# Tokens' statistics in parts, the last attention steps in another order, and no fills behind GpSimd's gathers

## What is computed

```python
def ffn(x, Wr, br, W1, b1, W2, b2):            # xf: 4096 tokens x 128
    expert = argmax(xf @ Wr.T + br, -1)
    h = relu(einsum('td,efd->etf', xf, W1) + b1[:, None, :])    # 8 experts, 512 wide
    y = einsum('etf,edf->etd', h, W2) + b2[:, None, :]
    return y[expert, arange(4096)]
def attn(x, wq, wk, wv, wproj, g_rms):
    q, k, v = heads of x @ wq.T, x @ wk.T, x @ wv.T
    q, k = rope(g_rms * q / rms(q)), rope(g_rms * k / rms(k))
    return softmax(q @ k.T / sqrt(8) + 1) @ v @ wproj.T
x = x + 0.5 * ffn(layernorm(x)); x = x + attn(layernorm(x)); x = x + 0.5 * ffn(layernorm(x))
```

## Time and profile before

| | |
|---|---|
| median of 3 runs | 461.86 us (461.74 to 462.61) |
| the profiled execution | 463.23 us, its span 461.4 us |
| PE busy | 419.0 us, 91% of the span |
| DVE busy | 374.3 us, 81% |
| ACT busy | 350.3 us, 76% |
| POOL busy | 327.3 us, 71% |
| stages by the timeline | routing to 33; pass 1 to about 140; steps 0 to 64 to about 378; pass 2 to 457; last scatter lands at the end |

### The profile page before, as it was taken

The page is one execution under the profiler, slowest core; times in us unless marked ns, Lnnn a source line. Parts: engine busy times, 40 slices in busy tenths (PEclk is TensorE's granted clock), DMA queues, the critical chain, the costliest instruction groups (busy, mean ns, idle before and its releaser), DMA issues.

```text
span 461.4 us, 13980 instructions
## 1 busy us (share of the span) xinstructions
PE 419.0 (91%) x4123; PEld 313.4 (68%) x4123; DVE 374.3 (81%) x992; ACT 350.3 (76%) x815; POOL 327.3 (71%) x528
## 2 busy tenths in 40 slices
PE   7889999989888899999999999999888989999996
PEld 4347999878665555655656556656555549998996
DVE  4895787998797788888898888998887786876774
ACT  4416777787756798999999889998777877776773
POOL 8019898888857879868687477557967634677756
PEclk9999999999999899999999999999999999999999
DMA  7882334252100000000000000000001122133310
GB/s 208 264 298 58 84 97 148 70 175 63 31 26 11 14 26 9 14 9 14 14 9 9 3 1 4 5 3 1 20 28 44 37 67 62 54 104 100 97 40 22
DMA packets 28649, 27.02 MB, mean 59 GB/s; under 512 B 5684, under 2 KB 25947, under 8 KB 28018
## 3 DMA queue, kind: packets, MB, share of 16 engines
q1 hardware_dynamic: 24034, 17.65, 12.9%
q0 software_dynamic: 4544, 8.49, 6.8%
HBM read 16.56 MB, written 12.71 MB: 63 GB/s over the span
## 4 chain that ended last, share of the span: by engine, by line
PE 48%; DVE 22%; issue 13%; ACT 8%; DMA 3%; POOL 2%; DVEq 1%; SPq 1%; POOLq 1%; ACTq 0%
PE PS L932 10%; PE PS L916 10%; DVE Smax L1897 9%; PE PS L1063 7%; PE PS L1016 5%; PE PS L1039 5%; ACT Pt L1306 3%; PE PS L998 3%; PE PS L982 3%; DVE St L1463 2%; PE PS L905 2%; PE PS L1093 1%; ACT QkT L1200 1%; DVE HsT L1740 1%; DMA XX<-x 1%
## 5 line engine op out<-in xcount | busy, mean ns | idle before, releaser
L1897 DVE TENSOR_REDUCE Smax<-PS 128x4 f32<-128x1024 f32 x128 | 156.1, 1224 | 32.2 <-PE PS L1016 31.2
L1306 ACT ACTIVATE Pt<-PS 128x1024 f32<-128x1024 f32 x128 | 126.2, 1024 | 18.5 <-PE PS L1039 15.3
L932 PE MATMUL PS<-W,HsT 128*128 x624 | 84.1, 278 | 2.0 <-DVE Ys L1751 2.0
L916 PE MATMUL PS<-XsT,Ws 128*128 128x128 f32 x624 | 83.2, 276 | 0.7 <-ACT XsT L1200 0.5
L916 PEld LDWEIGHTS PS<-XsT,Ws 128*128 128x128 f32 x624 | 76.4, 192 | 4.3 <-ACT XsT L1200 1.4
L932 PEld LDWEIGHTS PS<-W,HsT 128*128 128x128 f32 x624 | 76.1, 192 | 4.3 <-issue 3.4
L1063 PE MATMUL PS<-Pt,Vg 128*32 128x256 f32 x1024 | 68.5, 385 | 0.5 <-DVE Lg L1919 0.3
L730 POOL TENSOR_TENSOR HL<-Rn,Zero 128x512 fp32r<-128x512 f32 x28 | 35.4, 1284 | 37.5 <-DVE Rn L1880 35.9
L1016 PE MATMUL PS<-QkT 24*128 24x256 f32 x512 | 59.6, 305 | 1.9 <-DVE Smax L1897 1.7
L638 POOL DMA_INDIRECT Pt<-rows,TokI x39 | 40.5, 1038 | 28.4 <-DVE TokI L1692 19.8
L1016 PEld LDWEIGHTS PS<-QkT 24*128 24x128 f32 x512 | 40.0, 184 | 27.6 <-ACT Pt L1306 22.8
(11 more groups left out here) (277 smaller groups left out, 727.7 us busy)
## 6 DMA issues: line engine op xcount, KB each, us to landing
AtCol<-slots SPq DMA_DIRECT2D x39, 65.5 KB, 1.8
rows<-XX SPq DMA_DIRECT2D x8, 288.0 KB, 4.3
XX<-x SPq DMA_DIRECT2D x8, 256.0 KB, 4.5
W<-w1T SPq DMA_DIRECT2D x2, 1024.0 KB, 6.1
W<-w2T SPq DMA_DIRECT2D x2, 1024.0 KB, 9.1
mid<-mid_second SPq DMA_DIRECT2D x1, 1472.0 KB
mid<-Ys SPq DMA_DIRECT2D x16, 64.0 KB
QkT<-NmaxT SPq DMA_DIRECT2D x64, 4.0 KB
```

What stands on the lines that cost most here:

```text
L916: last = nc.tensor.matmul(PS[:, h_bank(n) + c // 2, (c % 2) * P:(c % 2 + 1) * P], Ws[:, n % R_WS, c * P:(c + 1) * P], XsT[:, n % 2, :], st ...
L932: last = nc.tensor.matmul(PS[:, y_bank(n), 0:P], HsT[:, n % 2, c, :], W2[:, ds(e * D_FF + c * P, P)], start=(c == 0), stop=(c == FC - 1))
L1306: nc.scalar.activation(Pt[:, m % 2, 2 * pair:2 * pair + 2, :, :].rearrange("p h c t -> p (h c t)"), PS[:, score_bank(m, pair):score_bank(m ...
L1897: nc.vector.tensor_reduce(Smax[:, b % 2, :, at:at + 33:32].rearrange("p t h -> p h t"), PS[:, max_bank(m, pair):max_bank(m, pair) + 2, :]. ...
```

## The change

`pause`, `Unread` and the semaphore `paused` go: 71 fills on POOL. On ACT the third copy of `Ws` in pass 1 comes behind the relu of tile 0. The layernorm of lot 5 goes from DVE to POOL. Two of the four statistics of lots 5, 7, 8 and 9 are taken a step ahead of the other two, and from sequence 7 on `xn` is taken in two parts at two other steps (n of 3 and of 2 modulo 4, where both were at 0). `inverse_deviation` of lots 6 to 9 goes from between the two exponentials of steps 10, 18, 26 and 34 to the end of the steps before. The tables of lots 0 and 1 go to other steps, and tiles are stored by another `STORE_AT`. In the last steps six matmuls that only filled a wait go, the values of 57 come ahead of the maxima's transpose, and from 61 on the first pair of scores comes a step ahead, with two more waits on ACT. The first `Ws` copies of pass 2 go from DVE to POOL. In pass 2 step 68 on DVE goes ahead in its tile and lot 3's routing to earlier tiles.

```diff
-LARGEST_AT = {38: 0, 48: 1, 59: 2}
-TIES_AT = {39: 0, 49: 1, 59: 2}
-PICK_AT = {42: 0, 50: 1, 59: 2}
-SEEN_AT = {43: 0, 51: 1, 59: 2}
-RANK_AT = {45: 0, 52: 1, 62: 2}
-POOL_SLOT_AT = {45: 0, 54: 1, 62: 2}
+LARGEST_AT = {38: 0, 50: 1, 59: 2}
+TIES_AT = {39: 0, 51: 1, 59: 2}
+PICK_AT = {42: 0, 51: 1, 59: 2}
+SEEN_AT = {44: 0, 52: 1, 59: 2}
+RANK_AT = {48: 0, 54: 1, 62: 2}
+POOL_SLOT_AT = {48: 0, 54: 1, 62: 2}
...
-STORE_AT = {45: (0,), 47: (1, 2), 48: (3, 4), 50: (5, 6), 51: (7, 8), 52: (9, 10), 53: (11,),
+STORE_AT = {48: (0, 1), 49: (2,), 50: (3, 4), 51: (5, 6, 7), 52: (8, 9), 53: (10, 11),
...
-FILL_MAXIMA = {58: 6}
+LAST_PROJECT = 3
+LAST_MAXIMA, SCORES_AHEAD = 58, 61
...
-LAST = {"norm": 0, "inverse": 5, "rank": 9}
+LAST = {"norm": 0, "inverse": 4, "rank": 8}
...
+XN_PARTS = 7
...
-        ROOT_BETWEEN = {8 * c - 22: c + 2 for c in range(4, N_CHUNK)}
-        POOL_LOTS = 6
+        ROOT_LATE = {8 * c - 23: c + 2 for c in range(4, N_CHUNK)}
+        POOL_LOTS = 5
+        FIRST_STATS = {0: 5, **{8 * c - 27: c + 2 for c in range(5, N_CHUNK)}}
...
-pauses = [0]
...
-def pause(columns=PAUSE):
...
-    if pauses[0]:
-        pool.wait_ge(paused, pauses[0])
-    nc.gpsimd.memset(Unread[:, 0:columns], 0.0).then_inc(paused, 1)
-    pauses[0] += 1
...
-    pause()
...
-    pause()
...
+def first_weights():
+    pool.wait_ge(slots_ready, 2)
+    for t in range(R_WS):
+        n = S_TILES + t
+        e = pool.value_load(tile_expert(1, t), min_val=0, max_val=N_EXP - 1)
+        nc.gpsimd.tensor_copy(Ws[:, n % R_WS, :], W1[:, ds(e * D_FF, D_FF)]).then_inc(ws_ready, 1)
+        nc.gpsimd.tensor_copy(Bs[:, bias(n), :], B1T[:, ds(e * FC, FC)]).then_inc(bs_ready, 1)
...
+    if n == WEIGHTS_AT:
+        first_weights()
...
-def scores(m):
-    b, g = divmod(m, N_GRP)
+def score_products(m, heads):
+    for c in range(SEQ_TILES):
+        for h in heads:
+            rows = slice(32 * h, 32 * h + SPLIT + 1)
+            last = nc.tensor.matmul(PS[:, score_bank(m, h // 2) + h % 2, c * T:(c + 1) * T],
+                                    QkT[rows, m % R_QK, 1, c * P:(c + 1) * P],
+                                    QkT[rows, m % R_QK, 0, :], start=True, stop=True)
+    return last
...
+def rows_ready(m):
...
-    def products(heads):
-        for c in range(SEQ_TILES):
-            for h in heads:
-                rows = slice(32 * h, 32 * h + SPLIT + 1)
-                last = nc.tensor.matmul(PS[:, score_bank(m, h // 2) + h % 2, c * T:(c + 1) * T],
-                                        QkT[rows, m % R_QK, 1, c * P:(c + 1) * P],
-                                        QkT[rows, m % R_QK, 0, :], start=True, stop=True)
-        return last
...
+def first_scores(m):
+    rows_ready(m)
+    score_products(m, (0, 1)).then_inc(score_ps, 1)
...
+def second_scores(m):
+    pe.wait_ge(exp_ready, 2 * m)
+    score_products(m, (2, 3)).then_inc(score_ps, 1)
...
+def scores(m):
...
-        products((0, 1)).then_inc(score_ps, 1)
-        pe.wait_ge(exp_ready, 2 * m)
-        products((2, 3)).then_inc(score_ps, 1)
+        if m < SCORES_AHEAD:
+            first_scores(m)
+        second_scores(m)
+        if SCORES_AHEAD <= m + 1 < N_ALL:
+            first_scores(m + 1)
...
+        rows_ready(m)
...
-        products(range(GH)).then_inc(score_ps, 2)
+        score_products(m, range(GH)).then_inc(score_ps, 2)
...
+    elif m == SCORES_AHEAD - 1:
+        last.then_inc(values_ps, 1)
...
-    if n in FILL_MAXIMA:
-        fill_const(FILL_MAXIMA[n], bank_of("nmaxT", seq(n, 2)))
...
+    if n == LAST_MAXIMA:
+        values(n - 1)
...
-    if group(n - 1):
+    if group(n - 1) and n != LAST_MAXIMA:
...
-        for t in range(1, R_WS):
-            w_copy(t)
+        w_copy(1)
...
-            if k and t == LAST["inverse"]:
-                inverse_deviation(N_LOT + len(ROUTE_LOTS))
...
+            if not k and t == 0:
+                w_copy(2)
...
+                if t == LAST["inverse"]:
+                    inverse_deviation(N_LOT + len(ROUTE_LOTS))
...
+    if pair == 0 and m == SCORES_AHEAD + 1:
+        act.wait_ge(values_ps, 1)
+    elif pair == 0 and m >= SCORES_AHEAD:
+        act.wait_ge(*filled("yu", m // 2 - 1))
...
-    if not late(n) and n not in FILL_MAXIMA:
+    if not late(n) and n != LAST_MAXIMA:
...
-    if n in ROOT_BETWEEN:
-        inverse_deviation(ROOT_BETWEEN[n])
...
-    if n in FILL_MAXIMA:
+    if n == LAST_MAXIMA:
...
+    if n in ROOT_LATE:
+        inverse_deviation(ROOT_LATE[n])
...
-    def weights():
-        for t in range(R_WS):
-            n, e = K0 + t, number(t)
-            nc.vector.tensor_copy(Ws[:, n % R_WS, :], W1[:, ds(e * D_FF, D_FF)]).then_inc(ws_ready, 1)
-            nc.vector.tensor_copy(Bs[:, bias(n), :], B1T[:, ds(e * FC, FC)]).then_inc(bs_ready, 1)
...
+            if k and t == LAST_PROJECT:
+                step(*DRAIN[t])
...
-                if t > 1:
+                if 1 < t < LAST_PROJECT:
...
+def reload_first(i):
+    dve.wait_ge(mid_in[i], 16 * (LOT[i].stop - LOT[i].start))
+    for j in range(LOT[i].start, LOT[i].start + 2):
+        nc.vector.bn_stats(St[:, j, :], X[:, j, :])
...
+def reload_rest(i):
+    stats(slice(LOT[i].start + 2, LOT[i].stop), lot_stats)
...
+def xn_part(b, tt):
+    j = SEQ_TILES * b + tt
+    if tt:
+        dve.wait_ge(ln_rstd, lot(j) + 1)
+        dve.wait_ge(*filled("turn", N_GRP * (b - 2) - 17))
+    part = nc.vector.scalar_tensor_tensor(out=XN[:, j % (2 * SEQ_TILES), :], in0=X[:, j, :], scalar=Mean[:, j:j + 1],
+                                          in1=Rstd[:, j:j + 1].to_broadcast([P, P]),
+                                          op0=ALU.subtract, op1=ALU.mult)
+    if not tt:
+        part.then_inc(xn_seq, 1)
...
-    elif seq(n, 20) >= 0:
+    elif 0 <= seq(n, 20) < XN_PARTS:
...
+    if n in FIRST_STATS:
+        reload_first(FIRST_STATS[n])
...
-        reload(STATS_AT[n])
+        if STATS_AT[n] in FIRST_STATS.values():
+            reload_rest(STATS_AT[n])
+        else:
+            reload(STATS_AT[n])
...
+    if seq(n, 21) >= XN_PARTS:
+        xn_part(seq(n, 21), 1)
...
-    if n == WEIGHTS_AT:
-        weights()
...
+    if seq(n, 18) >= XN_PARTS:
+        xn_part(seq(n, 18), 0)
...
-    if (t, place) == (9, 0):
+    if (t, place) == (8, 2):
...
-    if (t, place) == (9, 2):
+    if (t, place) == (9, 0):
...
```

## The result

In 20 runs of each the changed kernel took 459.76 us (458.61 to 463.42) and the kernel before 462.69 us (461.74 to 465.2); the ratio is 0.9945, with a 95% interval of 0.9927 to 0.9963. So it is faster, by 2.5 us (0.55% of 461.86; the two medians are 2.9 us apart) and not by 5.75. Ratios leave out executions over 1.5% above the fastest of the same kernel, medians and ranges do not. Profiled executions: 463.23 us before, 459.41 us after, 3.8 us apart. First the page of the kernel after: span, busy times, PE's granted clock.

A forecast was written before the change was run, and what follows sets the result against it. PE, busy in most of the span, and its loop of scores, exponentials and maxima were taken to bound the kernel; the terms summed to -5.75 us, from 461.86 to 456.1 us, with a range of 452.0 to 460.5.

The forecast's parts named there:

- The clock: Steps 0 to 3: PE's granted clock no longer falls once the 0.66 us wait goes, about 1.5 us of the -2.1.
- Last steps: Weights and filling matmuls go but POOL comes 2.57 us late: -0.2 us, from -2.4 if on time to +1.0.
- DVE's part in steps 0 to 3: DVE earlier at the maxima, so PE's 0.66 us wait goes: -0.6 us without the clock's part.
- The bound of -3.2: Steps 0 to 3: the most to be gained, if the steps come down to 3.75 us each.
- Roots: `inverse_deviation` moved from between the exponentials to the end of the step before, four times 0.19 us: -0.8, between -0.4 and -1.0.
- `xn` in parts: Statistics and `xn` in parts even DVE's load over a sequence's four steps: 0 us, with 0.7 to either side.
- Tables: Table operations of lots 0 and 1 at other steps, around 44 to 54: -0.65 us, bounds 0 and -1.0.
- Start, ramp, pass 2: Third `Ws` copy later at pass 1's start -0.4 us; fills gone in the ramp -0.5; tile 19's stall in pass 2 -1.1.
- Signs: What the profile after would show, such as a clock of 1.00 between 149 and 157 and ACT's Ln waiting on POOL.
- The fills: Removing 71 fills wins 21 us on POOL, nearly nothing of it on the path; -0.5 us taken for the ramp.
- Rival 3: Slower: the fills kept DVE free, without them DVE hits POOL's DMAs more often, 0.57 us each; 463 us; chance 0.05.
- Rival 2: The clock still falls and the last steps cost: 457.6 to 459.2 us, 460.5 with the tables at nothing; chance 0.25.

The follow-up runs named there:

- before_nofills: The kernel before without its two `pause()` calls, so without the 71 fills, nothing else changed: 461.76 us, ratio 0.9986 to the kernel before.
- lot5_dve: Changed kernel with tables and stores of lots 0 and 1 as before, sequence 15's `xn` in one piece, lot 5's layernorm on DVE: 456.30 us, ratio 0.9875.
- xn_whole: The changed kernel with every sequence's `xn` in one piece instead of parts: 459.65 us, ratio 0.9935 to the kernel before.
- old_lots: The changed kernel with the tables and storing steps of lots 0 and 1 as in the kernel before: 458.13 us, ratio 0.9897 to the kernel before.
- after_again: The changed kernel itself, run and profiled once more: 459.73 us, ratio 0.9949 to the kernel before.

## Why the prediction was wrong

- **Direction and range held**: faster, and 459.76 us is within 452.0 to 460.5. The size didn't: -2.5 us against -5.75, under half.
- **The clock, the failing step.** The prediction took the fall of the clock in step 2 to follow from PE's wait of 0.66 us there, counted its end with that wait as -1.5 us of the -2.1 for steps 0 to 3, and took this off the median. The runs show neither. `before_nofills` has the same wait (0.57 us) and a clock of 1.00 behind it, so the fall is a thing of that execution. And the medians of the kernel before hold little of it: of its executions beside the later runs, on three chips, those with a mean clock of 0.998 or more took between 0.8 us less and 0.5 us more than those at 0.990 to 0.997, by groups of runs. In the profile the 1.33 us went as said (step 2 took 5.87 us with the lower clock, 4.54 in `before_nofills`), but the changed kernel loses as much or more elsewhere: 1.3 us in the last steps in one profile, 2.7 us in steps 4 and 5 in the other. My estimate: freed of its 1.33 us, the profiled execution before is 461.90 us, 0.8 under its median; freed of 1.34 us, the one after is 458.07, 1.7 under its median. So by this estimate the clock adds 0.9 us more to the median than before, where 1.5 were to be won. That is 2.4 of the 2.8 us that are missing between medians; all other terms together gave 3.8 us (0.2 of it the start, which varies) where 4.25 were said.
- **Last steps**, the second miss: -0.2 was said, +1.85 came in the profile, +0.5 at full clock. Its first half was right: POOL late by 2.57 us (it came to 5.75 - 3.29 = 2.46), the Ln waiting for it, the weights' place taken by the late logits, nothing lost at the start of pass 2. What was mis-sized is the Ln: 0.4 us was worked out from ACT's place before, but ACT came earlier itself, as the filling matmuls ahead of it were gone, so it waited 0.99. And the sum ended at "less the 0.4 us". It didn't follow the wait on to ACT's exponentials and PE's idle of 1.74 us behind them.
- **DVE's part in steps 0 to 3**: -0.6 was said for PE's wait. From 4.54 to 4.16 us, 0.38, is what the statistics in parts give (`before_nofills`, `lot5_dve`; both at full clock), and the layernorm on POOL takes back 0.15: ACT waits 0.32 us for POOL, which was said to have time for it. The bound of -3.2 "if the steps come down to 3.75 each" was a wrong sum; from 17.12 us that is -2.1, the value taken.
- **Roots**: -0.8 said. The four steps took 0.31, 0.35, 0.33 and 0.17 us less, 1.16; other changes fall in these steps too, and no run takes the roots apart. **`xn` in parts**: 0 said, -0.24 and +0.74 measured in the two stretches (`xn_whole`). **Tables**: -0.65 said. From `old_lots` to the changed kernel, which differ in the tables and stores alone, steps 36 to 56 went from 79.72 to 79.13, -0.59: right, and hidden in the -0.05 by the parts of `xn`.
- **Start, ramp, pass 2**: -0.4, -0.5 and -1.1 said, -1.03 for the first two and -1.08 for the last. Right in size. But kernels that are the same in pass 1 and the ramp, without fills, took 104.35 to 105.06 us there, so the -1.03 doesn't show each of the two terms, and PE's wait at the first up-product was 0.37 us after, not under 0.2. In pass 2 the stall of tile 19 gave 1.39 us, and the tiles ahead, into which lot 3's routing moved, took back 0.3.
- **Signs**: no L631, a clock of 1.00 between 149 and 157, steps 10, 18, 26 and 34 as short as their neighbours or shorter, the Ln waiting on POOL, no wait on `slots` in tile 19: all came. The one for the clock told nothing, as the clock fell at 363 instead.
- **The fills**: right in that their removal gave little by itself (0.6 us here and in `before_nofills`). Missed was that the move of lot 5's layernorm needs it: with fills that move makes the change slower than the kernel before, by 0.3%. Rival 3 (fills keep DVE free) is refuted: no run without them is slower.
- **Rival 2** had the right shape, last steps that cost and a clock that still falls, and its band, 457.6 to 459.2, is nearest to the result; I gave it 0.25.

## What to carry to other kernels

An engine that a change makes late has more than one customer: follow the wait through each of them and on to the engine behind, rather than charging the first. Moving work to an engine that is idle on average costs what its queue delays: nine stores in a row, or two fetches ahead of a small result, each cost more than the move gave. And a stretch at the lower clock in one profile is no fixed cost of a place, and no saving to be counted off a median: compare first what many executions took, with their mean clocks.

## What the runs showed of the hardware

- The granted clock falls in different stretches in executions of the same kernel (158 to 165 us in one, 363 to 371 in another). Neither follows from the length of PE's wait ahead: 1.87 us at 367 in `after_again` had a clock of 1.00 behind it, and from 157 on the clock fell in four profiles and stayed at 1.00 in others, all with a wait of 0.74 or 0.75 us there. A stretch of some 7 us cost 2.7 us in steps 4 and 5 and 1.3 us in the last steps, where PE waits anyway.
- A copy of 128x512 float32 took 0.61 us on GpSimd and 0.43 on VectorE. The prediction had 0.6 as the lower bound and reckoned up to 1.28.
- Beside a GpSimd split VectorE's two-input operation took up to 1.13 us more (1.39 against 0.26), which made one step 1 us longer.
